# Self-attention in strips: where the reciprocals of the row sums are made and spread, and how many buffers hold them

## The chip, the cores and the metric

The kernel runs on one core of a Trainium2 chip. The metric is device time in microseconds, the median of several runs. TensorE is called PE, VectorE DVE, ScalarE ACT, GpSimd POOL, and SP is the engine that issues most DMAs. Times inside the kernel are from one profiled execution, counted from the start of its span.

## What is computed

A decoder layer on x of shape (8, 256, 512): self-attention, cross-attention and a mixture of experts, each behind a layer norm and added to x. The change touches the self-attention alone. Cut to that part:

```python
x = x + _L0_attn_ref(_layernorm(x), w_qkv, w_out)      # 16 heads of 32
    q, k, v = (qkv[:, :, 0], qkv[:, :, 1], qkv[:, :, 2])
    scores = jnp.einsum('bqhd,bkhd->bhqk', q / scale, k)
    scores = jnp.where(causal_mask[None, None], scores, NEG)
    attn = jax.nn.softmax(scores, axis=-1)
    out = jnp.einsum('bhqk,bkhd->bqhd', attn, v).reshape(b, s, HIDDEN)
    return out @ w_out
...
```

## The kernel before

The self-attention goes through the 8 batches (n) one by one, and each batch through 16 slots (h), one per head. Heads are taken in groups of four (HG). All five engines run the same list of slots, each at its own pace; what an engine does in a slot is set by lags: work with lag L that belongs to head t is done in slot t + L, and from slot 16 on in the first slots of the next batch. The order on an engine is fixed by the code; semaphores alone tie the engines together.

Per head: DVE adds the mask to the scores, negates and scales them into `prob` and takes the row maximum (L596, lag 0). POOL makes `shift` from it (L326, lag 0), ACT the exponentials and the row sums `rsum` (L397, lag 0). POOL rounds them to the upper float16 part (L333, lag 1), DVE takes the lower part (L604, lag 2), and SP issues the transposing DMA into `pt` (L255, lag 2).

Per group of four heads, on its last head's lags: PE makes all four heads' scores in the slot of the first head (L472), which waits until the maxima of the group before are read (`mx_done`), since there are only four score buffers. DVE takes the reciprocals of the row sums (`rinv`, L619, RINV_LAG), POOL spreads each over the 32 columns of its head (`rinv_wide`, L341, WIDE_LAG). PE multiplies the probabilities by v (L495, AV_LAG 7) and right behind that turns the spread reciprocals with an identity into the layout of the output (L502), for which it waits on `wide_done`. ACT copies them out of PSUM (L411), DVE multiplies the output by them (L614, lag 8), ACT rounds (L417, lag 9) and POOL takes the lower part `ot_lo` (L347, OT_LAG 9).

Between those, PE does one job in most slots: projections of q, k and v (`q`, `k`, `u`, `w`), the transposes X0 and X1 of the normalised input in slot 8, and the output products y0 and y1 in slots 10 and 11, which wait for `ot_done` of all four groups of the batch before. q0, k0, q1, k1 in slots 12 to 15 are already those of the next batch. A job's result is evacuated by ACT and, a slot later, by DVE (L575, y by L568), and three PSUM banks hold jobs, so a job waits until DVE has emptied the one three before it. POOL rounds v's lower parts two slots behind the job (L308, L310).

So PE's order in four slots is: scores, two jobs, values (L495), the turned reciprocals (L502), two jobs. Slot 10 holds the values of the batch's group 0, slot 14 those of group 1, slots 2 and 6 of the next batch those of groups 2 and 3. There is one buffer `rinv_wide`, which POOL refills after PE has read it (`r_done`).

Of the kernel before, what the change touches and what calls it, by code (L numbers as in the profile page):

```python
# [20 lines left out]
P = 128  # L21
B, S, D = 8, 256, 512
DC = D // P
TB = S // P
NT = B * TB
H, HD = 16, 32
HG = P // HD
# [8 lines left out]
def free_ap(ap, offset, dims):  # L36

    return bass.AP(tensor=ap.tensor, offset=ap.offset + offset, ap=[list(ap.ap[0])] + dims)


def wait(engine, semaphore, value):

    if not isinstance(value, int) or value > 0:
        engine.wait_ge(semaphore, value)
# [18 lines left out]
def self_attention(nc, ident, x, w_qkv, w_out, x1, xin, xr, x1_out, x1_last_out, x1_first_in,  # L63
# [9 lines left out]
    with ExitStack() as cx:  # L73
        sb = lambda n, s, d=F32: cx.enter_context(nc.sbuf_tensor(n, s, d))
# [18 lines left out]
        p_part = sb("p_part", [P, NPROB, 2, 3 * P], F16)  # L93
        pt = sb("pt", [P, NPT, 2 * 3, P], F16)
        rsum, rinv = sb("rsum", [P, G, TB, HG]), sb("rinv", [P, G, TB, HG])
        rinv_wide = sb("rinv_wide", [P, TB, HG, HD])
        o_sb = [sb(f"a_o_sb{i}", [P, S]) for i in range(2)]
        ot_hi, ot_lo = sb("ot_hi", [P, G, S], F32R), sb("ot_lo", [P, G, S], F32R)
        raw = sb("a_raw", [P, 4, DC, D])
# [16 lines left out]
        rinv_done, wide_done, av_done, r_done, rs_done = (sem(n) for n in (  # L116
            "rinv_done", "wide_done", "av_done", "r_done", "rs_done"))
# [9 lines left out]

        BANK = {j: i % 3 if i < JOBS - 1 else 1 for i, j in enumerate(ORDER)}

        HI_LAG, LO_LAG, DMA_LAG, RINV_LAG, WIDE_LAG, AV_LAG, R_LAG, ON_LAG, OT_HI_LAG, OT_LAG = 1, 2, 2, 5, 6, 7, 7, 8, 9, 9  # L130
        LO_JOB_LAG, PARTS_LAG = 1, 2

        PASSES = ((0, 0), (1, 0), (0, 1), (1, 1), (2, 0))
# [87 lines left out]
        def v_half(j):  # L221
            return slice(0, D // 2) if j[0] == "u" else slice(D // 2, D)
# [63 lines left out]
        @block.gpsimd  # L286
        def _(pool):
            nc.gpsimd.memset(expo[:], -0.5).then_inc(consts, 1)
            nc.gpsimd.memset(ident[:], 0.0).then_inc(consts, 1)
            nc.gpsimd.memset(mask[:], 0.0).then_inc(consts, 1)  # L290
            pool.wait_ge(consts, 3)
            nc.gpsimd.affine_select(out=ident[:], in_=ident[:], compare_op=ALU.not_equal, fill=1.0, base=0,
                                    pattern=[[-1, P]], channel_multiplier=1).then_inc(consts, 1)

            nc.gpsimd.affine_select(out=mask[:, P:], in_=mask[:, P:], compare_op=ALU.is_ge, fill=NEG, base=0,
                                    pattern=[[-1, P]], channel_multiplier=1).then_inc(consts, 1)

            def next_rstd(k):

                pool.wait_ge(ln_dve, k * 5 + 5)  # L300
                nc.gpsimd.tensor_tensor(rstd[:], veps[:], expo[:], ALU.pow).then_inc(ln_rstd, 1)

            def v_lower_parts(j, n):

                i, half, before = int(j[1]), v_half(j), v_at(j, n)
                pool.wait_ge(job_ev, job_at(j, n) + 1)
                pool.sem_inc(tick_pool, 1)
                nc.gpsimd.tensor_copy(v_part[1][:, i, half], v_rest[:, i, :]).then_inc(v_mid_done, 1)  # L308
                pool.wait_ge(v_mid_done, before + 1)
                nc.gpsimd.tensor_tensor(v_part[2][:, i, half], v_rest[:, i, :], v_part[1][:, i, half],  # L310
                                        ALU.subtract).then_inc(v_done, 1)

            def out_weights(c):
                if c == 0:
                    pool.wait_ge(w_in[3], 16)
                nc.gpsimd.tensor_copy(wo_hi[:, c, :], raw[:, 3, c, :]).then_inc(wo_hi_done, 1)
                pool.wait_ge(wo_hi_done, c + 1)
                nc.gpsimd.tensor_tensor(wo_lo[:, c, :], raw[:, 3, c, :], wo_hi[:, c, :].bitcast(F32),
                                        ALU.subtract).then_inc(wo_split, 1)

            def slot(n, h):
                e = head_at(h, 0, n)
                if e is not None:
                    pool.wait_ge(mx_done, n * H + h + 1)
                    pool.sem_inc(tick_pool, 1)
                    nc.gpsimd.tensor_scalar(shift[:, e, :], nmax[:, e, :], LN_UNIT, None, ALU.add).then_inc(shift_done, 1)  # L326
                t = head_at(h, HI_LAG, n)
                if t is not None:
                    pool.wait_ge(ex_done, n * H + h - HI_LAG + 1)
                    pool.sem_inc(tick_pool, 1)  # L330
                    wait(pool, pt_in[t % HG], groups_before(h, HI_LAG, n) * 16)
                    pool.sem_inc(tick_pool, 1)
                    nc.gpsimd.tensor_copy(p_part[:, t % NPROB, 0, :], prob[:, t % NPROB, :]).then_inc(p_hi_done, 1)  # L333
                g = group_at(h, WIDE_LAG, n)
                if g is not None:
                    before = groups_before(h, WIDE_LAG, n)
                    wait(pool, r_done, before)
                    pool.sem_inc(tick_pool, 1)
                    pool.wait_ge(rinv_done, before + 1)
                    pool.sem_inc(tick_pool, 1)  # L340
                    nc.gpsimd.tensor_copy(rinv_wide[:], free_ap(rinv[:, g, :, :], 0, [[HG, TB], [1, HG], [0, HD]]))\  # L341
                        .then_inc(wide_done, 1)
                g = group_at(h, OT_LAG, n)
                if g is not None:
                    pool.wait_ge(ot_hi_done, groups_before(h, OT_LAG, n) + 1)
                    pool.sem_inc(tick_pool, 1)
                    nc.gpsimd.tensor_tensor(ot_lo[:, g, :], o_sb[g % 2][:], ot_hi[:, g, :].bitcast(F32),  # L347
                                            ALU.subtract).then_inc(ot_done, 1)
                for j, of in jobs_before(h, PARTS_LAG, n):
                    if j[0] in "uw":  # L350
                        v_lower_parts(j, of)
                if h == 3 and head_at(h, 0, n) is not None and (not isinstance(n, int) or n < B - 1):
                    next_rstd(n + 1)
                if isinstance(n, int) and n == 0 and h in WO_LATER:
                    out_weights(WO_LATER[h])

            next_rstd(0)
            for h in range(H):
                slot(0, h)
            with pool.Fori(1, B - 1) as n:  # L360
                for h in range(H):
                    slot(n, h)
            for n in (B - 1, B):
                for h in range(H):
                    slot(n, h)
# [63 lines left out]
        def _(pe):  # L429
# [48 lines left out]
            def values(g, h, n):  # L478

                before, of = groups_before(h, AV_LAG, n), n if h >= AV_LAG else n - 1  # L480
# [19 lines left out]
                pe.wait_ge(wide_done, before + 1)  # L500
                for q in range(TB):
                    m = nc.tensor.matmul(o_ps[:, 1, q * P:(q + 1) * P],  # L502
                                         rinv_wide[:, q, :, :].rearrange("p j d -> p (j d)"), ident[:],
                                         start=True, stop=True)
                m.then_inc(r_done, 1)

# [1121 lines left out]
```

## Time and profile before

| | us |
|---|---|
| median of 3 runs | 865.14 |
| lowest, highest | 862.89, 865.21 |
| the profiled execution | 865.61 |
| its span, first to last instruction | 863.9 |

Busy in the span: PE 700.5 us (81%), PE weight loads 620.7, DVE 507.3 (59%), ACT 311.4, POOL 311.7 (36% each). The self-attention takes about the first 405 us, the cross-attention and the experts the rest. The second batch's first scores start at 67 us, and from there to the last batch each takes 45 us.

How to read it: a line of a timeline gives the start, the time from the first start to the last end of equal neighbours (x4 means four instructions), the engine, the line, what is written from what, and in brackets how long the engine sat idle before it and which instruction ended that. A matmul helper records its work under L58, so tiles tell one product from another. [...] A matmul's record reaches past the start of the next one, so the difference of two starts, not the length, is what one takes in a row of equal ones.

### The profile page before, as it was taken

Reading aid. Unit: us, or ns where it says so; the run is one execution under the profiler, and the core shown is the slowest. Engines: PE = TensorE matmul, PEld = TensorE weight load, DVE = VectorE, ACT = ScalarE, POOL = GpSimd, SP = SyncE. Lnnn points to the kernel's source line nnn. Section 1 sums busy time; section 2 is a strip of 40 time slices with the busy share of each in tenths; the row PEclk is TensorE's granted clock in tenths of the full one; section 3 lists DMA queues with packets and bytes.
Section 4 is the critical chain, followed back from the end, with each engine's and each line's share of the span. In section 5 each row is a group of like instructions: output and inputs, shape, how many; then the busy total and the mean of one; then the engine's idle time right before and its main releaser. Section 6 shows DMA issues by size and latency. Waiting matters only on the chain. (4 is left out here: it accounts for less than half of the span.)

```text
span 863.9 us, 19090 instructions
## 1 busy us (share of the span) xinstructions
PE 700.5 (81%) x6040; PEld 620.7 (72%) x6041; DVE 507.3 (59%) x1456; ACT 311.4 (36%) x984; POOL 311.7 (36%) x534
## 2 busy tenths in 40 slices
PE   5578787868686869665989999999999998509995
PEld 5468676858576767544878889888898997407884
DVE  4587574757666575542856465554646555554664
ACT  3455363545545454531432323131322324312221
POOL 0565454454646363641610010101010114545662
PEclk9789998989998999976799999999999999758999
DMA  9166463545454444741942131212223124516630
GB/s 345 48 109 84 86 126 79 130 89 121 97 112 97 105 80 88 133 107 51 353 180 98 50 98 49 97 51 94 73 73 98 48 73 141 152 43 203 198 120 24
DMA packets 142885, 95.07 MB, mean 110 GB/s; under 512 B 110846, under 2 KB 115070, under 8 KB 142720
## 3 DMA queue, kind: packets, MB, share of 16 engines
q1 hardware_dynamic: 137184, 82.00, 36.6%
q0 software_dynamic: 5664, 12.61, 4.7%
q8 instruction: 19, 0.31, 0.2%
q14 instruction: 18, 0.15, 0.1%
HBM read 56.14 MB, written 18.77 MB: 87 GB/s over the span
## 5 line engine op out<-in xcount | busy, mean ns | idle before, releaser
L397 ACT ACTIVATE prob<-prob,shift 128x128 f32<-128x128 f32 (+1 forms) x256 | 114.5, 449 | 170.4 <-POOL shift L326 170.4
L58 PE MATMUL b_bank<-w_hi 128*128 128x256 f32 (+1 forms) x576 | 119.9, 331 | 7.2 <-DVE w_lo L1187 7.2
L999 ACT CAST w_hi<-b_bank 128x256 fp32r<-128x256 f32 (+1 forms) x144 | 60.2, 445 | 161.0 <-PE b_bank L58 143.2
L58 PE MATMUL b_bank<-w_lo,w_hi 128*128 128x256 f32 (+1 forms) x576 | 114.8, 322 | 0.0
L58 PE MATMUL b_bank<-w_hi,w_lo 128*128 128x256 f32 (+1 forms) x576 | 114.7, 322 | 0.0
L596 DVE CUSTOM_DVE_ANT_0 prob<-a_s,mask 128x128 f32<-128x128 f32 (+1 forms) x256 | 79.2, 347 | 49.2 <-PE a_s L472 48.9
L604 DVE TENSOR_TENSOR p_part<-prob,p_part 128x384 f16<-128x384 f32 x128 | 79.7, 622 | 42.9 <-POOL p_part L333 42.7
L58 PEld LDWEIGHTS b_bank<-w_hi 128*128 128x128 f32 x576 | 90.1, 196 | 15.7 <-DVE w_lo L1187 7.8
L58 PEld LDWEIGHTS b_bank<-w_lo,w_hi 128*128 128x128 f32 x576 | 90.8, 194 | 8.0
L1187 DVE TENSOR_TENSOR w_lo<-b_bank,w_hi 128x256 fp32r<-128x256 f32 (+1 forms) x144 | 68.4, 508 | 47.4 <-ACT w_hi L999 47.3
L58 PEld LDWEIGHTS b_bank<-w_hi,w_lo 128*128 128x128 f32 x576 | 90.7, 194 | 7.6
L326 POOL TENSOR_SCALAR shift<-nmax 128x2 f32<-128x2 f32 x128 | 42.4, 332 | 137.5 <-DVE nmax L596 126.7
L502 PE MATMUL a_o<-ident,rinv_wide 128*128 128x128 f32 x128 | 27.9, 351 | 68.3 <-POOL rinv_wide L341 68.3
L502 PEld LDWEIGHTS a_o<-ident,rinv_wide 128*128 128x128 f32 x128 | 20.7, 230 | 75.8 <-POOL rinv_wide L341 75.5
L333 POOL CAST p_part<-prob 128x384 f16<-128x384 f32 x128 | 64.3, 503 | 8.7 <-ACT prob L397 0.7
L58 PE MATMUL a_job<-a_xt_hi,wqkv_hi 128*128 128x256 f32 x256 | 45.4, 301 | 7.9 <-DVE q_part L575 2.8
L397 ACT ACTIVATION_READ_ACCUMULATOR prob<-prob,shift 128x1 f32 x256 | 48.1, 188 | 0.0
L955 POOL TENSOR_TENSOR b_rstd<-b_veps,b_expo 128x2 f32<-128x2 f32 x8 | 6.1, 757 | 112.9 <-DVE b_veps L1165 112.9
L58 PEld LDWEIGHTS a_job<-a_xt_hi,wqkv_hi 128*128 128x128 f32 x256 | 35.6, 196 | 12.1 <-DVE wqkv_lo L560 4.2
L347 POOL TENSOR_TENSOR ot_lo<-a_o_sb,ot_hi 128x256 fp32r<-128x256 f32 x32 | 25.0, 781 | 47.3 <-ACT ot_hi L417 47.3
L58 PE MATMUL a_job<-a_xt_lo,wqkv_hi 128*128 128x256 f32 x256 | 41.0, 284 | 0.0
L58 PE MATMUL a_job<-a_xt_hi,wqkv_lo 128*128 128x256 f32 x256 | 40.9, 283 | 0.0
(169 smaller groups left out, 1360.0 us busy)
## 6 DMA issues: line engine op xcount, KB each, us to landing
stage<-in_w SPq DMA_DIRECT2D x8, 1024.0 KB, 5.5
xin<-in_x SPq DMA_DIRECT2D x8, 512.0 KB, 4.1
xr<-in_x SPq DMA_DIRECT2D x8, 512.0 KB, 4.2
x<-xr SPq DMA_DIRECT2D x8, 512.0 KB, 3.2
xin<-x SPq DMA_DIRECT2D x8, 512.0 KB, 4.6
b_cin_t<-in_ctx_t SPq DMA_DIRECT2D x8, 512.0 KB, 3.6
b_cin<-in_ctx SPq DMA_DIRECT2D x8, 512.0 KB, 3.5
xr<-x SPq DMA_DIRECT2D x8, 512.0 KB
```

The source lines that it names most:

```text
L58: ins = pe_matmul(out, a, b, start=first and i == 0, stop=last and i == len(steps) - 1)
L326: nc.gpsimd.tensor_scalar(shift[:, e, :], nmax[:, e, :], LN_UNIT, None, ALU.add).then_inc(shift_done, 1)
L333: nc.gpsimd.tensor_copy(p_part[:, t % NPROB, 0, :], prob[:, t % NPROB, :]).then_inc(p_hi_done, 1)
L347: nc.gpsimd.tensor_tensor(ot_lo[:, g, :], o_sb[g % 2][:], ot_hi[:, g, :].bitcast(F32), ALU.subtract).then_inc(ot_done, 1)
L397: a = nc.scalar.activation(prob[:, e % NPROB, cols], prob[:, e % NPROB, cols], ACT.Exp, scale=-1.0, bias=shift[:, e, q:q + 1], accum_out=r ...
L502: m = nc.tensor.matmul(o_ps[:, 1, q * P:(q + 1) * P], rinv_wide[:, q, :, :].rearrange("p j d -> p (j d)"), ident[:], start=True, stop=True)
L596: m = nc.vector.tensor_tensor_reduce(out=prob[:, s % NPROB, cols], in0=s_ps[s % HG][:, q, 0:P * (q + 1)], in1=mask[:, P * (1 - q):], scale ...
L604: nc.vector.tensor_tensor(p_part[:, t % NPROB, 1, :], prob[:, t % NPROB, :], p_part[:, t % NPROB, 0, :], ALU.subtract).then_inc(p_done, 1)
L955: nc.gpsimd.tensor_tensor(rstd[:, 0, :], veps[:, 0, :], expo[:], ALU.pow).then_inc(ln_rstd, 1)
L999: nc.scalar.copy(hi, src).then_inc(job_hi, 1)
L1187: nc.vector.tensor_tensor(lo, src, hi.bitcast(F32), ALU.subtract).then_inc(job_ev, 1)
```

## The change

Three things, all in `self_attention`.

1. RINV_LAG goes from 5 to 2 and WIDE_LAG from 6 to 3. The last head of a group has number 3, 7, 11 or 15, so DVE takes the reciprocals in slots 1, 5, 9, 13 and not in 0, 4, 8, 12 of the group after, and POOL spreads them in slots 2, 6, 10, 14 that follow the group at once, where it had done so in slots 1, 5, 9, 13 one group later.
2. `rinv_wide` becomes two buffers, taken in turn by the group's number.
3. POOL's copy waits for `r_done` of one group fewer, since the buffer it fills was read two groups ago.

AV_LAG stays 7: PE reads the spread values where it did.

```diff
-        rinv_wide = sb("rinv_wide", [P, TB, HG, HD])
+        rinv_wide = [sb(f"rinv_wide{i}", [P, TB, HG, HD]) for i in range(2)]
...
-        HI_LAG, LO_LAG, DMA_LAG, RINV_LAG, WIDE_LAG, AV_LAG, R_LAG, ON_LAG, OT_HI_LAG, OT_LAG = 1, 2, 2, 5, 6, 7, 7, 8, 9, 9
+        HI_LAG, LO_LAG, DMA_LAG, RINV_LAG, WIDE_LAG, AV_LAG, R_LAG, ON_LAG, OT_HI_LAG, OT_LAG = 1, 2, 2, 2, 3, 7, 7, 8, 9, 9
...
-                    wait(pool, r_done, before)
+                    wait(pool, r_done, before - 1)
                     pool.sem_inc(tick_pool, 1)
                     pool.wait_ge(rinv_done, before + 1)
                     pool.sem_inc(tick_pool, 1)
-                    nc.gpsimd.tensor_copy(rinv_wide[:], free_ap(rinv[:, g, :, :], 0, [[HG, TB], [1, HG], [0, HD]]))\
+                    nc.gpsimd.tensor_copy(rinv_wide[g % 2][:], free_ap(rinv[:, g, :, :], 0, [[HG, TB], [1, HG], [0, HD]]))\
                         .then_inc(wide_done, 1)
...
-                                         rinv_wide[:, q, :, :].rearrange("p j d -> p (j d)"), ident[:],
+                                         rinv_wide[g % 2][:, q, :, :].rearrange("p j d -> p (j d)"), ident[:],
```

On POOL, in the loop's slots 5 and 6, the old place of the copy and the new one. Each pair of L326 and L333 is one head: shift of this slot, upper part of the head before. L308 and L310 are v's lower parts.

```order
@@ -91,8 +92,8 @@
 L44 ISA
 L333 CAST p_part<-prob 128x384
-L341 COPY rinv_wide<-rinv 128x256
-L324 REGISTER_ALU
-L326 TENSOR_SCALAR shift<-nmax 128x2
-L333 CAST p_part<-prob 128x384
+L324 REGISTER_ALU
+L326 TENSOR_SCALAR shift<-nmax 128x2
+L333 CAST p_part<-prob 128x384
+L341 COPY rinv_wide<-rinv 128x256
 L306 REGISTER_ALU
 L308 CAST v_part<-v_rest 128x256
```

The copy moved from behind slot 5's upper part to behind slot 6's, so it now stands right ahead of v's lower parts. It belongs to another group too: in slot 6 it is that of heads 0 to 3, in slot 5 it had been that of the batch before's heads 12 to 15.

On DVE, in the loop's slots 4 and 5; L596 and its reads are a head's maximum, L604 the lower part, L575 an evacuation.

```order
@@ -178,13 +178,13 @@
 L570 REGISTER_ALU
 L575 TENSOR_TENSOR k_part<-a_job,k_part 128x256
+L596 ISA prob,nmax<-a_s,mask 128x128
+L596 ISA nmax 128x1
+L596 ISA prob,nmax<-a_s,mask 128x256
+L596 ISA nmax 128x1
+L604 TENSOR_TENSOR p_part<-prob,p_part 128x384
+L570 REGISTER_ALU
+L575 TENSOR_TENSOR v_rest<-a_job,v_part 128x256
 L618 ISA
 L619 RECIPROCAL rinv<-rsum 128x8
```

The reciprocals moved one head back within the four slots, from ahead of the second head's maximum to ahead of the third's.

## Rows read from the trace of the kernel before

**Rows 1.** The list of waits, 0 to 450 us: us in total, times, longest us

```profile
PE a_o L502 <- POOL rinv_wide L341: 68.3, 31, 5.2
```

**Rows 2.** Busy time by stretch: PE, PEld, DVE, ACT, POOL, then granted clock, DMA

```profile
195.00:240.00 45.00, 35.80 (x456) 31.60 (x456) 29.56 (x111) 22.37 (x86) 23.24 (x49) 0.96 0.48 105
```

**Rows 3.** Timeline of PE, one batch: start us, length us, line, work, [idle before]

```profile
203.99 0.96 PE L472 MATMUL a_s<-k_part,q_part 32*128 32x128 f32 x24
...
210.28 0.71 PE L502 MATMUL a_o<-ident,rinv_wide 128*128 128x128 f32 x4 [0.83 <-POOL rinv_wide L341]
...
213.75 0.96 PE L472 MATMUL a_s<-k_part,q_part 32*128 32x128 f32 x24
...
220.25 0.71 PE L502 MATMUL a_o<-ident,rinv_wide 128*128 128x128 f32 x4 [1.59 <-POOL rinv_wide L341]
...
223.72 0.96 PE L472 MATMUL a_s<-k_part,q_part 32*128 32x128 f32 x24
...
225.63 1.01 PE L495 MATMUL a_o<-pt,v_part 128*32 128x256 f16 x40
231.72 1.22 PE L502 MATMUL a_o<-ident,rinv_wide 128*128 128x128 f32 x4 [5.08 <-POOL rinv_wide L341]
232.60 2.05 PE L58 MATMUL a_job<-wout_hi,ot_hi 128*128 128x512 f32 x4
...
235.59 1.08 PE L58 MATMUL a_job<-wout_hi,ot_lo 128*128 128x512 f32 x4
...
239.35 0.96 PE L472 MATMUL a_s<-k_part,q_part 32*128 32x128 f32 x24
...
245.59 0.71 PE L502 MATMUL a_o<-ident,rinv_wide 128*128 128x128 f32 x4 [1.41 <-POOL rinv_wide L341]
...
248.97 0.96 PE L472 MATMUL a_s<-k_part,q_part 32*128 32x128 f32 x24
```

**Rows 4.** Timeline of DVE, the same batch

```profile
219.88 0.72 DVE L604 TENSOR_TENSOR p_part<-prob,p_part 128x384 f16<-128x384 f32 x1 [0.93 <-POOL p_part L333]
...
222.00 0.08 DVE L596 DVE_READ_ACCUMULATOR2_ANT nmax<- 128x1 f32 x1
...
246.81 0.08 DVE L596 DVE_READ_ACCUMULATOR2_ANT nmax<- 128x1 f32 x1
...
257.73 0.08 DVE L596 DVE_READ_ACCUMULATOR2_ANT nmax<- 128x1 f32 x1
```

**Rows 5.** Timeline of POOL, the same batch

```profile
219.80 0.40 POOL L341 COPY rinv_wide<-rinv 128x256 f32<-128x256 f32 x1
...
224.03 0.68 POOL L310 TENSOR_TENSOR v_part<-v_rest,v_part 128x256 bf16<-128x256 f32 x1
225.84 0.35 POOL L326 TENSOR_SCALAR shift<-nmax 128x2 f32<-128x2 f32 x1 [1.13 <-DVE nmax L596]
...
228.65 0.73 POOL L347 TENSOR_TENSOR ot_lo<-a_o_sb,ot_hi 128x256 fp32r<-128x256 f32 x1 [1.90 <-ACT ot_hi L417]
```

**Rows 6.** The same, one microsecond of the first batch

```profile
54.00:55.00 1.00, 0.03 (x1) 0.03 (x1) 1.00 (x5) 0.96 (x4) 0.94 (x4) 0.50 1.11 82
```

**Rows 7.** Timeline of PE, first batch

```profile
54.97 1.22 PE L502 MATMUL a_o<-ident,rinv_wide 128*128 128x128 f32 x4 [2.27 <-POOL rinv_wide L341]
56.34 1.66 PE L472 MATMUL a_s<-k_part,q_part 32*128 32x128 f32 x24
...
63.80 0.71 PE L502 MATMUL a_o<-ident,rinv_wide 128*128 128x128 f32 x4 [0.60 <-POOL rinv_wide L341]
```

**Rows 8.** Timeline of PE, last batch

```profile
359.89 0.96 PE L472 MATMUL a_s<-k_part,q_part 32*128 32x128 f32 x24
...
367.09 1.22 PE L502 MATMUL a_o<-ident,rinv_wide 128*128 128x128 f32 x4 [5.22 <-POOL rinv_wide L341]
...
375.26 0.96 PE L472 MATMUL a_s<-k_part,q_part 32*128 32x128 f32 x24
...
383.76 1.79 PE L495 MATMUL a_o<-pt,v_part 128*32 128x256 f16 x40 [1.73 <-DMA pt<-p_part]
```
## The prediction

> **Names.** A batch of the self-attention has 16 slots, one per head. Slots 0 to 3 are strip A, 4 to 7 strip B, 8 to 11 strip C, 12 to 15 strip D. Each strip opens on PE with the scores of its four heads (L472). "S" is the start of those scores; a strip's length runs from its S to the next one.
>
> **What bounds the kernel now.** I read the list of waits of the first 450 us first. PE stood for 68.3 us in 31 waits before the matmuls of L502, the ones that turn the spread reciprocals, and POOL's copy of L341 ended all of them [rows 1]. The busy times by stretch say whether that engine matters there: in a stretch of 45 us, which is one batch, PE is busy 35.80 us, DVE 29.56, POOL 23.24, ACT 22.37 [rows 2]. PE idles 9.2 us of a batch, so a wait of PE is time as long as nothing else is nearly as full. Then the timeline of PE, strip by strip [rows 3]: before L502 it waits 0.83 us in strip A, 1.59 in B, 5.08 in C and 1.41 in D, 8.9 us together, which is all of its idle time but 0.3. Strip lengths are A 9.76 us (203.99 to 213.75), B 9.97 (to 223.72), C 15.63 (to 239.35), D 9.62 (to 248.97), 44.98 together. The work queued behind the waiting matmuls, two projections or the two output products and then the next scores, is what starts late, and with the scores DVE's next four heads.
>
> **What the change removes.** The copy for a group now stands four slots and more before PE asks for it: POOL makes it in slot 2 of the strip before, PE reads it in slot 2 of the next. POOL can't be that far behind, since PE's next scores themselves wait for the last head's maxima of the strip before. So the wait at L502 goes in every strip, and the question is what is late next. Two things are, and I work both out for each strip: PE's own work (length less the wait), and DVE's last maximum of the strip, for which the next scores wait, plus about 0.15 us until they start (in the first batch the maximum was the later one, and the scores began at 56.34 [rows 7]).
>
> Strip A: PE 9.76 - 0.83 = 8.93. DVE: the last maximum is read at 257.73 + 0.08, that is S + 8.84 for S = 248.97 [rows 3, 4], so 9.0. I take 8.95: **0.8 us less**.
>
> Strip B: PE 9.97 - 1.59 = 8.38; DVE 222.00 + 0.08 - 213.75 = 8.33, with the hand-over 8.5 [rows 3, 4]. **1.5 less**. Both limits are within 0.15 us of each other: from here on more speed on PE alone would bring nothing.
>
> Strip D: PE 9.62 - 1.41 = 8.21; DVE 246.81 + 0.08 - 239.35 = 7.54. PE's last projection needs a bank that DVE empties one head earlier than the last; that comes some 0.2 us too late for the shorter strip, an estimate from the same timeline. I take 8.4: **1.2 less**.
>
> Strip C is where most lies, and where not all of it can be had. Without the wait PE does the copy's matmuls right behind the values, and then the output product of L454 waits for the lower part of the attention's output, L347 on POOL, which ended at 228.65 + 0.73 = 229.38, S + 5.66 [rows 3, 5]. Before, that was hidden behind the later wait. It also comes a little later against S: POOL's head shift at 225.84 had waited 1.13 us for DVE; it now comes 1.45 us earlier (strip B's gain), while POOL is held until 224.71 by the lower parts of v (224.03 + 0.68), and by 0.25 us more, because the moved copy of 0.40 us stands ahead of them and only some 0.15 us of it falls into time in which POOL waited for the exponential [rows 5]. So shift starts 0.6 us later after S, and the product at S + 5.66 + 0.6 + 0.1 = 6.35. The two products took 6.75 us (232.60 to 239.35) at a clock that had fallen in the wait of 5.08 us; at the full clock four matmuls take 0.94 us (235.59 to 239.35 are four such rows), six rows 5.64 [rows 3]. So strip C is 12.0 us long with the full clock (3.6 less) and 13.1 with the low one (2.5 less). PE would stand some 2.2 us before the product. [...] I take the middle, **3.0 less**.
>
> **The sum.** A batch is 0.8 + 1.5 + 3.0 + 1.2 = 6.5 us shorter, and there are six whole ones (slot 0 of the second to slot 0 of the eighth): 39 us. In the eighth, A and B give 2.3, and of C's wait of 5.22 us [rows 8] about 1.1 stays before the product, since it needs L347 all the same: 4.1. Its strip D gives nothing: from S = 375.26 the chain goes through the last heads and their transposing DMAs, and PE waits for pt at 383.76 [rows 8]. The first batch gives 0.6 of strip D [rows 7] and nothing of C, whose scores began at 56.34 although the wait had ended 1.4 us earlier: they waited for the maximum. 39 + 2.3 + 4.1 + 0.6 = **46 us**. What comes behind the self-attention starts from its end and is the same. The profiled execution took 865.61 us (span 863.9), so 819.6; the median of the three runs is 0.5 lower, 819.1. I say 819.
>
> **Costs beside it.** The reciprocal (a slot later in its strip, 0.19 us) stays ahead of the same last maximum, and its input is long there: zero, at most 0.1 us a strip. The copy's new wait (r_done of the group before last) is met a whole strip before. The copy no longer stands ahead of POOL's shift of slot 2, and stands ahead of the one of slot 3: from -0.4 to +0.4 us on one head's chain, 31 times, -12 to +12 us, if that chain were the only limit. I take zero, since in A and B the heads of slot 2 and 3 are followed by DVE's own work until the maximum, and in C and D PE is the limit. The transposing DMAs move with the heads. Of v's lower parts the first values of a batch need the second one; it comes at S + 2.7 in strip C, 0.6 us after PE could use it, before the longer wait for L347, so it costs nothing.
>
> One row bears on that bound. DVE's lower part of slot 2 took 0.72 us at 219.88 and had started beside the copy of 219.80 [rows 4, 5]. [...]
>
> **Rivals.** *B: the heads' chain takes the wait over.* DVE's idle time at the start of a strip now lets it finish the strip before. Shorter strips could push that work (lower part, an evacuation, the product with the reciprocals) past the end of the scores, and POOL with it. For it: the two limits of A and B are nearly equal already, and DVE waited 0.93 us for POOL inside strip B [rows 4]. Against it: DVE is busy 29.56 of 45 us [rows 2]. If A, B and D lose another 1.0 us each, seven batches give 21 us back: 840. *C: no change.* The label names the last of several things, and the transposed probabilities or v come at the same time: 865. Against it: behind the values nothing but the copy is left for L502, and values ran 5 us ahead in strip C [rows 3]. *D: slower.* The copy stands ahead of slot 3's shift and of v's lower parts on POOL. If the PE wait is only moved to the next scores, as in the first batch's strip C [rows 7], each strip pays the copy: 32 x 0.40 = 12.8 us, 878. It decides as soon as the last maximum, not PE, ends every strip and POOL's copy lies on its path. *E: more.* Full clock in every strip C and no loss anywhere: 7.1 x 6 + 7.5 = 50, and 3 us from shorter stretches of low clock behind it: 812.
>
> **How the numbers follow.** Forecast 0.66 (813 to 827), B 0.18, E 0.07, C 0.05, D 0.04. The range leaves out C, D and the slower part of B: 808 to 838, where 838 is B with nine tenths of its price. A measurement here tells 0.3%, 2.6 us, from no change. Faster: 0.66 + 0.18 + 0.07 = 0.91 and nothing of C; same 0.05; slower 0.04.
>
> **What would show it.** PE's waits for rinv_wide gone from the list of waits, in the list in their place: PE for ot_lo, about 2.2 us in each strip C, and scores that wait for the last maximum in A and B. Lengths of A 8.95, B 8.5, C 12.0 to 13.1, D 8.4, a batch 38 to 39 us. The granted clock in strip C says which of the two lengths holds. POOL's L308 behind L341 in slot 2 of strip B. The forecast is wrong if batches stay above 41 us; then the row before the scores names what took over.

## The result, and the profile after

| | us | of before |
|---|---|---|
| before, median of 4 | 864.85 (862.89 to 865.21) | |
| changed, median of 4 | 822.42 (819.07 to 825.95) | 0.9514, 95% interval 0.9469 to 0.9559 |
| changed, the profiled execution | 825.95, span 824.2 | |

The kernel became 42 us faster. The profiled execution is the slowest of its four, which turns out to matter below.

In the list of PE's groups over the first 410 us, the matmuls of L502 have lost their whole idle time (0.0 us behind the bar, where [rows 1] had 68.3), and are shorter (311 ns each, where it had been 351). Of their 32 groups of four, ten took 1.14 to 1.22 us before, two take 1.22 now, and nearly all others take 0.71. The one of [rows 3] with 1.22 us, at 231.72, ran at a granted clock of 0.50, counted as a share of full speed:

```profile
L502 PE MATMUL a_o<-ident,rinv_wide 128*128 128x128 f32 x128 | 23.8, 311 | 0.0
```

What PE waits for in their place, in the list of waits of the first 410 us (total, times, longest):

```profile
PE a_job L58 <- POOL ot_lo L347: 14.1, 8, 2.3
...
PE a_o L495 <- DMA pt<-p_part: 10.3, 2, 6.0
...
PE a_o L495 <- POOL v_part L310: 7.9, 8, 1.5
```

PE's values (L495) wait for the DMAs twice, at the end of the last batch. The page's table of costly groups has one more wait that matters here: DVE waits 32.2 us for POOL's upper part, where it had waited 42.7:

```profile
L604 DVE TENSOR_TENSOR p_part<-prob,p_part 128x384 f16<-128x384 f32 x128 | 80.8, 631 | 33.2 <-POOL p_part L333 32.2
```

One batch by its own stretch, from the scores of slot 0 to the next ones. PE is busy as long as before [rows 2], in 39.31 us, not 45, that is 91% of it (this is the shortest of the six batches):

```profile
189.11:228.42 39.31, 35.89 (x449) 31.45 (x448) 30.18 (x112) 22.14 (x87) 23.26 (x50) 0.96 0.54 120
```

PE's timeline of that batch, for [rows 3]. Strips begin at 189.11, 198.10, 206.46, 219.79 and 228.42:

```profile
189.11 0.96 PE L472 MATMUL a_s<-k_part,q_part 32*128 32x128 f32 x24
...
198.10 0.96 PE L472 MATMUL a_s<-k_part,q_part 32*128 32x128 f32 x24
...
206.46 0.96 PE L472 MATMUL a_s<-k_part,q_part 32*128 32x128 f32 x24 [0.17 <-issue]
...
209.33 1.01 PE L495 MATMUL a_o<-pt,v_part 128*32 128x256 f16 x40 [0.89 <-POOL v_part L310]
210.27 0.71 PE L502 MATMUL a_o<-ident,rinv_wide 128*128 128x128 f32 x4
212.78 2.07 PE L58 MATMUL a_job<-wout_hi,ot_hi 128*128 128x512 f32 x4 [1.80 <-POOL ot_lo L347]
214.65 1.55 PE L58 MATMUL a_job<-wout_lo,ot_hi 128*128 128x512 f32 x4
...
219.79 0.96 PE L472 MATMUL a_s<-k_part,q_part 32*128 32x128 f32 x24
...
226.85 0.74 PE L58 MATMUL a_job<-a_xt_hi,wqkv_hi 128*128 128x256 f32 x4 [0.16 <-DVE k_part L575]
...
228.42 0.96 PE L472 MATMUL a_s<-k_part,q_part 32*128 32x128 f32 x24
```

The reader is to see three things. L502 stands right behind the values now (210.27, and in the other strips without a wait). The output product waits for ot_lo until 212.78, 6.32 us after the scores at 206.46. And its first rows are long: 2.07 and 1.55 us for four matmuls that take 0.92 from start to start from 216.03 on.

All strips of the two profiled executions, worked out from the starts of L472 in such timelines; strip C is split at the start of the output products:

```
us            A (0-3)  B (4-7)   C until products + products      D (12-15)
before        9.6-9.8  9.9-10.0  8.8-8.9 + 6.8 to 8.2 (mean 7.4)   9.6
changed       9.0      8.35      6.3     + 7.0 to 8.6 (mean 7.9)   8.6
changed, eighth batch
              8.8      8.3       5.1     + 5.7
```

### The profile page after: what moved, and what is told of

Read it like the earlier page. It is cut to its first block and busy times, and to the rows that moved or that the text cites. A ratio compares the mean times of both kernels' runs of the same rounds, so it can differ in the third digit from the quotient of the medians.

```text
span 824.2 us, 19084 instructions
## 1 busy us (share of the span) xinstructions
PE 701.5 (85%) x6040; PEld 621.1 (75%) x6041; DVE 512.8 (62%) x1456; ACT 310.1 (38%) x984; POOL 311.8 (38%) x534
## 5 line engine op out<-in xcount | busy, mean ns | idle before, releaser
L604 DVE TENSOR_TENSOR p_part<-prob,p_part 128x384 f16<-128x384 f32 x128 | 80.8, 631 | 33.2 <-POOL p_part L333 32.2
L596 DVE CUSTOM_DVE_ANT_0 prob<-a_s,mask 128x128 f32<-128x128 f32 (+1 forms) x256 | 79.4, 347 | 34.2 <-PE a_s L472 34.1
L1187 DVE TENSOR_TENSOR w_lo<-b_bank,w_hi 128x256 fp32r<-128x256 f32 (+1 forms) x144 | 68.3, 507 | 46.1 <-ACT w_hi L999 46.0
L326 POOL TENSOR_SCALAR shift<-nmax 128x2 f32<-128x2 f32 x128 | 45.6, 356 | 98.2 <-DVE nmax L596 90.9
L333 POOL CAST p_part<-prob 128x384 f16<-128x384 f32 x128 | 64.3, 503 | 8.7 <-ACT prob L397 0.7
L495 PE MATMUL a_o<-pt,v_part 128*32 128x128 f16 (+1 forms) x1280 | 33.8, 254 | 18.2 <-DMA pt<-p_part 10.3
L955 POOL TENSOR_TENSOR b_rstd<-b_veps,b_expo 128x2 f32<-128x2 f32 x8 | 6.1, 756 | 111.2 <-DVE b_veps L1165 111.2
L495 PEld LDWEIGHTS a_o<-pt,v_part 128*32 128x32 bf16 x1280 | 26.0, 99 | 23.6 <-issue 20.3
L959 POOL TENSOR_TENSOR b_rstd<-b_veps,b_expo 128x2 f32<-128x2 f32 x8 | 5.6, 697 | 96.4 <-DVE b_veps L1165 96.3
L1468 ACT CAST c_xt_hi<-c_bank 128x512 fp32r<-128x512 f32 x23 | 13.5, 587 | 74.3 <-PE c_bank L1488 74.3
L347 POOL TENSOR_TENSOR ot_lo<-a_o_sb,ot_hi 128x256 fp32r<-128x256 f32 x32 | 23.4, 730 | 47.5 <-ACT ot_hi L417 47.5
```

Source lines behind the costliest of these rows:

```text
L495: m = nc.tensor.matmul(o_ps[j * HD:(j + 1) * HD, 0, seen], v_part[a][:, k, at:at + HD], pt[:, (g * HG + j) % NPT, 3 * z + blocks.start:3 * ...
L596: m = nc.vector.tensor_tensor_reduce(out=prob[:, s % NPROB, cols], in0=s_ps[s % HG][:, q, 0:P * (q + 1)], in1=mask[:, P * (1 - q):], scale ...
L604: nc.vector.tensor_tensor(p_part[:, t % NPROB, 1, :], prob[:, t % NPROB, :], p_part[:, t % NPROB, 0, :], ALU.subtract).then_inc(p_done, 1)
L1187: nc.vector.tensor_tensor(lo, src, hi.bitcast(F32), ALU.subtract).then_inc(job_ev, 1)
L1468: nc.scalar.copy(xt_hi[:, k % 2, :], t_ps[k % 2][:, :]).then_inc(xt_hi_done, 1)
```

## The experiments

All took the same inputs; unless a text says otherwise they compute the whole layer. Strips were read from each run's trace in the way of the table above.

### Which part of the change brings it

Both halves alone. First the new lags with one buffer:

```diff
-        HI_LAG, LO_LAG, DMA_LAG, RINV_LAG, WIDE_LAG, AV_LAG, R_LAG, ON_LAG, OT_HI_LAG, OT_LAG = 1, 2, 2, 5, 6, 7, 7, 8, 9, 9
+        HI_LAG, LO_LAG, DMA_LAG, RINV_LAG, WIDE_LAG, AV_LAG, R_LAG, ON_LAG, OT_HI_LAG, OT_LAG = 1, 2, 2, 2, 3, 7, 7, 8, 9, 9
```

> The new lags (2 and 3) with the one rinv_wide buffer of before, so POOL's copy waits until PE has read the copy of the group before. Theory 1 (the place of the copy is all that matters): PE reads at about 4.8 us after a strip's first scores and POOL reaches the copy at about 6.7 us in strip B, so the wait costs nothing and the time is that of the changed kernel, 822 us, within 2 us. Theory 2 (the second buffer is needed, since the copy now stands in the same slot as PE's read): PE and POOL wait for each other, the heads behind the copy come 0.5 us or more later in each of 31 groups, 838 us or more.

Measured: 823.16 us median (815.26 to 827.7), ratio 0.9542 (0.9495 to 0.9588). A 9.0, B 8.36, the products at 6.33, D 8.64, all as in the changed kernel. Theory 1 holds: the place of the copy is all, and the second buffer brings nothing that these runs can tell. POOL waited for PE to free the one buffer once, for 1.6 us, in the last batch.

Then two buffers with the lags of before:

> The lags of before (5 and 6) with two buffers in turn. Theory 1: nothing moves, PE's waits for rinv_wide stay at 68 us in 31 waits, and the time is that of before, 865 us, within 3. If the one buffer had held POOL back, these waits and the time would fall; the gain of two buffers alone would then be a part of the 42 us.

Measured: 864.47 us (one run) beside 864.51 of before, strips A 9.7, B 9.9, C 15.6 to 17.0, D 9.7, and 68.5 us in 31 waits of PE for rinv_wide. The buffer alone does nothing.

The run with one buffer also shows what its own median hides. Its products took 5.7 us in four of the six whole batches of the profiled execution (815.26 us) and 7.3 in the others, where the changed kernel's took 7.0 to 8.6 in all six (825.95 us). Everything else in the whole batches is the same to 0.05 us.

### What makes the output products of strip C long

Busy time by microsecond of the changed kernel's strip C; the granted clock is the figure behind POOL's count:

```profile
211.00:212.00 1.00, 0.00 (x0) 0.00 (x0) 1.00 (x2) 0.74 (x2) 0.07 (x1) 1.00 0.70 134
212.00:213.00 1.00, 0.22 (x1) 0.23 (x2) 0.89 (x6) 0.00 (x0) 0.99 (x2) 0.61 0.95 190
213.00:214.00 1.00, 1.00 (x3) 0.81 (x4) 0.00 (x0) 0.00 (x0) 0.85 (x2) 0.50 0.04 7
...
216.00:217.00 1.00, 1.00 (x6) 0.80 (x5) 0.20 (x1) 0.77 (x3) 0.94 (x3) 1.00 0.33 68
```

PE had ended L502 by 211.0 and stood until 212.78. The granted clock was 1.00 until 212.2, while PE stood, 0.50 from 212.3 on, 0.48 us before the products began, and 1.00 again at 216. So that PE has no such gap, the turning matmuls of group 0 are done five times over:

```diff
-                for q in range(TB):
+                for q in [0, 1] * (5 if g == 0 else 1):
                     m = nc.tensor.matmul(o_ps[:, 1, q * P:(q + 1) * P],
```

> The changed kernel, with the two turning matmuls of group 0 done five times over (same result), so that PE works through the 1.8 us in which it waits for ot_lo ahead of the output products of strip C. If the low granted clock there is what makes the two products take 7.0 to 8.6 us instead of 5.6, and it falls because of PE's idle time, strip C goes from 13.3 to 14.9 us down to 12 to 12.6 and the time to 808 to 814 us. If the clock falls all the same, the time stays at 822 to 824. If the products are long for another reason, such as waits for their operands, the records keep their length at granted clock 1.00.

Measured: 809.26 us (807.41 to 811.1), ratio 0.9361 (0.932 to 0.9401), 13 us under the changed kernel. PE's timeline of one strip C:

```profile
198.65 0.96 PE L472 MATMUL a_s<-k_part,q_part 32*128 32x128 f32 x24
...
202.46 2.50 PE L502 MATMUL a_o<-ident,rinv_wide 128*128 128x128 f32 x20
204.99 1.19 PE L58 MATMUL a_job<-wout_hi,ot_hi 128*128 128x512 f32 x4
206.01 1.08 PE L58 MATMUL a_job<-wout_lo,ot_hi 128*128 128x512 f32 x4
...
210.69 0.96 PE L472 MATMUL a_s<-k_part,q_part 32*128 32x128 f32 x24
```

The products start 6.34 us after the scores, as in the changed kernel, and take 5.7 us in all seven batches, at a granted clock of 1.00: 1.02 us from the first row's start to the second's, about 0.92 for the others. Strip C is 12.04 us in all six whole batches. The time that work without a result fills is not lost, since PE would have stood.

The same in the kernel before, with 20 products of the output weights into the bank that y0 overwrites, behind the values of group 0:

```diff
                 m.then_inc(av_done, 1)
+                if g == 0 and has("y0", n):
+                    pe.wait_ge(job_ev, job_at(*last_in_bank("y0", n)) + 1)
+                    for i in range(20):
+                        nc.tensor.matmul(bank("y0")[:, :], wo_hi[:, i % DC, 0:P], wo_hi[:, i % DC, :], start=True, stop=True)
                 pe.wait_ge(wide_done, before + 1)
```

> The kernel before, with 20 idle products of the output weights behind the values of group 0, into the bank that the output product overwrites, so that PE works through 4.5 of the 5.1 us in which it waits for rinv_wide in strip C. It splits the gain. If the low clock behind that wait costs what the spread of strip C says (15.6 to 17.0 us, of which 8.9 until the product starts, so 6.7 to 8.1 where full clock needs 5.6), strip C becomes 14.5 and the time 850 to 856 us: then 10 to 14 us of the distance between the kernel before and the one with the fed clock, 864.5 to 809.3, is clock and the rest waiting. If the filling work is too long or the bank comes late, strip C starts its product later than 8.9 us after its scores and the gain is smaller.

Measured: 847.69 us (845.89 to 850.12), ratio 0.9826 (0.9791 to 0.9861). Less than 2%, but clear of the seven runs of before beside it (860.88 to 866.7).

```profile
217.32 0.96 PE L472 MATMUL a_s<-k_part,q_part 32*128 32x128 f32 x24
...
220.17 4.83 PE L503 MATMUL a_job<-wout_hi 128*128 128x512 f32 x20
225.36 0.71 PE L506 MATMUL a_o<-ident,rinv_wide 128*128 128x128 f32 x4 [0.36 <-POOL rinv_wide L341]
225.83 1.17 PE L58 MATMUL a_job<-wout_hi,ot_hi 128*128 128x512 f32 x4
...
231.51 0.96 PE L472 MATMUL a_s<-k_part,q_part 32*128 32x128 f32 x24
```

Products of 5.69 us in all seven batches, at a granted clock of 1.00, against a mean of 7.4: 7 x 1.7 = 12 us. They start 0.37 us earlier, 2.6 us more: L502 takes 0.71 us at 225.36, at a granted clock of 1.00, where [rows 3] had 1.22. The whole was 16.3 us (864.0 to 847.7), a little more than I expected. The distance between the two kernels with PE fed is 847.7 - 809.3 = 38.4 us. That is what the change brings with the clock of strip C taken out of both, so it is waiting. Left to itself the change brings 42 us, since the kernel before loses 16.3 us to that clock and the changed one 13.2 (822.4 to 809.3).

### What ends strips A and B

```diff
                     dve.wait_ge(ex_done, before * HG + HG)
+                    nc.vector.reciprocal(rinv_again[:], rsum[:, g, :, :])
                     nc.vector.reciprocal(rinv[:, g, :, :], rsum[:, g, :, :]).then_inc(rinv_done, 1)
```

> The changed kernel, with each reciprocal on DVE done twice (the first into a spare tile). Theory: strips A and B now end with DVE's last maximum, C and D with PE. Then A grows from 9.00 and B from 8.36 by one reciprocal, 0.11 to 0.19 us, and C's start of the output product and D's 8.63 stay. Rival: PE's own work ends A and B too (its sum was 8.93 and 8.38); then A and B stay within 0.03 us.

Measured: 821.98 us (one run). A 9.00 and B 8.36 in every whole batch, products at 6.33, D 8.63. My expectation failed: one more reciprocal on DVE ahead of the last maximum moved nothing. That left PE, or a chain that DVE itself waits on. So PE was made lighter; this kernel leaves out one of the three passes of the projections:

```diff
-                                   ([w_hi[:, c, cols] for c in chunks], [w_lo[:, c, cols] for c in chunks]))
+                                   ([w_hi[:, c, cols] for c in chunks], [w_lo[:, c, cols] for c in chunks]), passes=2)
...
-                                   ([xt_hi[:, c, :] for c in chunks], [xt_lo[:, c, :] for c in chunks]))
+                                   ([xt_hi[:, c, :] for c in chunks], [xt_lo[:, c, :] for c in chunks]), passes=2)
```

> The changed kernel, with one of the three passes (lower part of the left operand times upper part of the right) left out of the projections of q, k and v, so those are less exact. Each is 0.45 us shorter, which takes 1.8 us of PE's work from strips A, B and D. Doubling the reciprocals on DVE had not moved A and B, so either PE ends them after all (then they fall to about 7.2 and 6.6 us and the time by over 20 us), or the heads' chain over POOL and ACT does, which had room for a second reciprocal while DVE waited for POOL (then A stays at 9.00 and B at 8.36 within 0.1, strip C's product still starts at 6.3, and D falls until its last maximum ends it, from 8.63 to about 7.7). By the second the time falls by 7 to 8 us at the same draws of the clock, and the granted clock may fall more often, since PE idles more.

Measured: 810.69 us (one run). A 8.99 and B 8.36 stay although PE has 1.8 us less to do in each, so PE does not end them. D fell to 8.17 only, since its last projection waits for the bank that DVE empties (k_part in the list below; 1.5 us in strip D). PE's starts of scores, and the waits of 60 to 300 us:

```profile
183.78 0.96 PE L473 MATMUL a_s<-k_part,q_part 32*128 32x128 f32 x24
...
192.77 0.96 PE L473 MATMUL a_s<-k_part,q_part 32*128 32x128 f32 x24 [1.50 <-DVE nmax L597]
...
201.14 0.96 PE L473 MATMUL a_s<-k_part,q_part 32*128 32x128 f32 x24 [2.00 <-issue]
```

```profile
PE a_s L473 <- DVE nmax L597: 9.0, 6, 1.5
...
PE a_job L59 <- DVE k_part L576: 14.5, 13, 1.6
```

The row at 201.14 names no releaser, but the last maximum's read ended 0.10 us ahead of it. So the heads' chain ends A and B. DVE's timeline of the changed kernel, whose scores start at 189.11 (A), 198.10 (B) and 206.46 (C), shows how it runs:

```profile
195.03 0.56 DVE L604 TENSOR_TENSOR p_part<-prob,p_part 128x384 f16<-128x384 f32 x1 [0.45 <-POOL p_part L333]
...
196.07 0.68 DVE L541 BATCH_NORM_STATS2 a_stats<-xin 128x6 f32<-128x512 f32 x1
196.67 0.41 DVE L548 BATCH_NORM_AGGREGATE a_mv<-a_stats 128x2 f32<-128x6 f32 x2
197.12 0.17 DVE L550 TENSOR_SCALAR a_veps<-a_mv 128x2 f32<-128x2 f32 x1
...
197.87 0.08 DVE L596 DVE_READ_ACCUMULATOR2_ANT nmax<- 128x1 f32 x1
...
203.99 0.56 DVE L604 TENSOR_TENSOR p_part<-prob,p_part 128x384 f16<-128x384 f32 x1
...
206.28 0.08 DVE L596 DVE_READ_ACCUMULATOR2_ANT nmax<- 128x1 f32 x1
```

The first row is slot 2 of strip A, with the wait for POOL (0.45 us) into which a second reciprocal disappears: in that run the wait is 0.39 and the row starts 5.92 us after the scores, as here. Behind it DVE works without a pause of more than 0.14 us until the last maximum, read 8.84 us after the scores; in strip B it is 8.26 us. The next scores start 0.15 and 0.10 us after the ends of these reads. So strip A ends by POOL until slot 2 and by DVE's own work behind it, and part of that work is the next batch's layer norm (L541 to L550, 1.24 us from 196.07 to 197.31, where the last maximum begins). The eighth batch tells this: it has no such rows, and with the lighter PE its A and B are 7.65 and 7.62 us. DVE in its strip A, whose scores start at 296.43:

```profile
302.30 0.56 DVE L605 TENSOR_TENSOR p_part<-prob,p_part 128x384 f16<-128x384 f32 x1 [1.05 <-POOL p_part L334]
...
303.90 0.08 DVE L597 DVE_READ_ACCUMULATOR2_ANT nmax<- 128x1 f32 x1
```

The lower part starts 5.87 us after the scores, as ever, but the last maximum's read ends 1.68 us behind it and not 2.92. So a reciprocal on DVE ahead of the wait for POOL costs nothing, and the layer norm behind it is what the strip's length holds.

### Where the copy is best placed

Twice the copy, the first into a spare tile, in slot 2:

> The changed kernel, with POOL's copy made twice (the first into a spare tile), 0.35 to 0.4 us more in slot 2 of each strip. If my account of its place holds, A, B and D stay (the copy lies behind the upper part for which DVE waits), the first batch's third strip, which ends with its last maximum, grows by 0.4, and in strip C the output product starts 0.35 to 0.4 later than 6.3 us after the scores, 7 times: 2.5 to 3 us in all. If the copy stood on the chain of all strips, the time grows by 31 x 0.4 = 12 us.

Measured: 818.3 us, one run, with products of 5.7 us, at a granted clock of 1.00, in four of seven batches; that clock is why the time lies under the changed kernel's, and the strips are what to compare. A 9.00, B 8.36 and D 8.63 stay; the products start at 6.85, not 6.33, and the first batch's third strip, which ends with its last maximum, is 8.72 us, not 8.11 to 8.26 as in the runs with one copy in slot 2. One more copy costs strip C 0.5 us, a little more than I expected, and the other strips of a whole batch nothing. POOL's timeline of the changed kernel, for [rows 5]:

```profile
205.13 0.40 POOL L341 COPY rinv_wide<-rinv 128x256 f32<-128x256 f32 x1
...
208.31 0.67 POOL L310 TENSOR_TENSOR v_part<-v_rest,v_part 128x256 bf16<-128x256 f32 x1
209.06 0.40 POOL L326 TENSOR_SCALAR shift<-nmax 128x2 f32<-128x2 f32 x1
...
211.93 0.72 POOL L347 TENSOR_TENSOR ot_lo<-a_o_sb,ot_hi 128x256 fp32r<-128x256 f32 x1 [1.90 <-ACT ot_hi L417]
```

The copy of slot 6 is at 205.13, v's lower part ends at 208.98, and shift of slot 8 starts 0.08 later: POOL is late for strip C, and L347 with it.

So the copy goes where POOL waits anyway, ahead of L347 in slot 0 of the next strip (lag 5), one buffer, and the reciprocal into slot 3 (lag 4):

```diff
-        HI_LAG, LO_LAG, DMA_LAG, RINV_LAG, WIDE_LAG, AV_LAG, R_LAG, ON_LAG, OT_HI_LAG, OT_LAG = 1, 2, 2, 5, 6, 7, 7, 8, 9, 9
+        HI_LAG, LO_LAG, DMA_LAG, RINV_LAG, WIDE_LAG, AV_LAG, R_LAG, ON_LAG, OT_HI_LAG, OT_LAG = 1, 2, 2, 4, 5, 7, 7, 8, 9, 9
```

> One buffer, reciprocals in slot 3 behind the last maximum (lag 4), copy in slot 0 of the next strip (lag 5), where POOL waits about 1.2 us for ot_hi. PE reads it in slot 2. If POOL's place of the copy matters as I argued (it delays v's lower parts and the shift of strip C), strip C becomes 0.3 us shorter than in the changed kernel and strips A and B 0.1 us, since the reciprocals leave the path to the maximum: 819 to 821 us. If lead is what counts, the copy comes at 3.5 us after the strip's start and PE asks at 3.8 to 4.8, so PE waits again in strip C, and the time is 823 or more.

Measured: 813.28 us (811.24 to 814.05), ratio 0.9405 (0.9366 to 0.9444), better than expected. The products start at 5.93, not 6.33, and kept the full clock in five of the six whole batches (5.7 us at a granted clock of 1.00, against 7.28 us at a mean of 0.77 in the sixth). A is 9.0. B is longer, 8.59, so the places of copy and reciprocal alone give some 0.2 us a batch (0.4 less in C, 0.2 more in B); most of the 9 us is the clock. PE's gap ahead of the products is 1.64 us here and not 1.80; that this is why the clock held more often is not shown. In B, L347 and DVE's L554 ran into each other; POOL first, DVE below:

```profile
192.99 0.40 POOL L341 COPY rinv_wide<-rinv 128x256 f32<-128x256 f32 x1
194.24 1.01 POOL L347 TENSOR_TENSOR ot_lo<-a_o_sb,ot_hi 128x256 fp32r<-128x256 f32 x1 [0.85 <-ACT ot_hi L417]
```

```profile
194.12 0.54 DVE L554 TENSOR_SCALAR a_xn<-xin,a_mv,a_rstd 128x512 f32<-128x512 f32 x1
```

L347 took 1.01 us, not 0.72, with L554 just started. In the kernel before it had been so too (the last section has the row). With the reciprocal back in slot 1, ahead of L554, and PE fed as above:

> One buffer, copy in slot 0 of the next strip (lag 5) as in the run with lags 4 and 5, reciprocals in slot 1 as in the changed kernel (lag 2), and PE kept busy before the output products by the repeated turning matmuls of group 0. With lags 4 and 5 strip C took 11.63 where the clock held and strip B 8.59, since POOL's L347 ran into DVE's L554 (1.01 us instead of 0.72). If it is the reciprocal ahead of L554 that lets L347 start first, strip B comes back to 8.36 and a batch takes 9.0 + 8.36 + 11.63 + 8.64 = 37.6: 805 to 807 us. If B stays at 8.6, 808.

Measured: 807.38 us (806.07 to 807.81), ratio 0.9347 (0.9315 to 0.9379). B is 8.36 again, C 11.63, the batch 37.64 us: 0.4 us less than the 38.04 of the fed kernel with the copy in slot 2, and 1.9 us less in all.

### What the output product waits for

L347 waits for ACT's rounding (L417), which stood behind the job's evacuation. Here it goes ahead of it, in all strips; else the changed kernel:

```diff
+                g = group_at(h, OT_HI_LAG, n)
+                if g is not None:
...
+                    nc.scalar.copy(ot_hi[:, g, :], o_sb[g % 2][:]).then_inc(ot_hi_done, 1)
                 for j in jobs_of(h, n):
                     if j not in LATE:
                         evac(j, n)
...
-                g = group_at(h, OT_HI_LAG, n)
-                if g is not None:
...
-                    nc.scalar.copy(ot_hi[:, g, :], o_sb[g % 2][:]).then_inc(ot_hi_done, 1)
```

> The changed kernel, with ACT rounding the attention's output (L417) ahead of the job's evacuation in the same slot. In strip C it stood behind the two transposed inputs (1.05 us). If L347 on POOL is what the output product of strip C waits for, the product starts at 5.3 to 5.5 us after the scores and not at 6.3, and PE's idle time there shrinks from 1.8 to about 0.8, so that the clock may stay up as well: 810 to 817 us. A and B: L347 also stands ahead of the upper part for which DVE waits 0.2 to 0.9 us, so they may gain 0.1. Rival: the transposed input's evacuation is needed first and C does not move; 820 or more.

Measured: 803.94 us (802.95 to 806.0), ratio 0.9314 (0.928 to 0.9349). PE's timeline of one strip C, whose scores start at 194.47:

```profile
197.20 1.01 PE L495 MATMUL a_o<-pt,v_part 128*32 128x256 f16 x40 [0.75 <-POOL v_part L310]
...
199.69 1.19 PE L58 MATMUL a_job<-wout_hi,ot_hi 128*128 128x512 f32 x4 [0.84 <-POOL ot_lo L347]
...
205.40 0.96 PE L472 MATMUL a_s<-k_part,q_part 32*128 32x128 f32 x24
```

The products start at 5.23, PE's gap ahead of them is 0.84 us and not 1.80, and they took 5.7 us in all seven batches, at a granted clock of 1.00, without any filling work. A became 8.84, B 8.32 and D 8.4: L347 stands on the chain ahead of slot 2's upper part. The time is below the 810 to 817 that I expected, which had only strip C move by 1 us and left the clock open. Both edits together:

> One buffer, reciprocals in slot 1 (lag 2), copy in slot 0 of the next strip (lag 5), and ACT's rounding of the output ahead of the evacuation. If the 0.4 us that the copy's place cost strip C is still there once the rounding is early, C goes from 10.93 to 10.5 us and the time from 804 to 801. If POOL then waits in slot 0 for nothing, so that the copy stands on the way to L347, C keeps 10.9 and A and B grow: 804 to 806.

Measured: 800.58 us (799.97 to 801.58), ratio 0.9269 (0.9234 to 0.9304). Products at 4.82, C 10.5, a batch 36.05 us. This is the best version run, 22 us under the changed kernel, with the one buffer of before.

## Why the prediction was right

The prediction was 819 us in a range of 808 to 838, and 822.4 was measured. Its forecast, not a rival, is what happened: the wait at L502 went, strips A, B, D and the start of the products came within 0.25 us of what was worked out for them, and PE waited for ot_lo in strip C. How near the time came is in part luck. The two profiled executions differ by 39.7 us, the medians by 42.4, and 46 was forecast; and two executions with the same strips but for the clock of strip C took 815.3 and 825.95 us. Point by point:

- **What bounds the kernel, and that the wait goes.** Right. 68.3 us of waits at L502 became 0.0, and 38.4 us of the gain is there with the low clock of strip C taken out of both kernels.
- **Strip A, 8.95.** 9.00 measured, by the last maximum, as the sum had it. The chain to it is POOL's until slot 2 and DVE's own work behind that, as the costs said; the reciprocal stands ahead of the wait for POOL, so that its cost is zero, as forecast, though not only because "its input is long there".
- **Strip B, 8.5.** 8.35. The last maximum was read at 8.26 us and not 8.33, and its hand-over took 0.10 us and not 0.15.
- **Strip C until the product, 6.35.** 6.32. The parts hold too: the values waited 0.89 us for v's lower parts, the product 1.80 us for L347, where the text has "some 2.2".
- **Strip C, the products.** Here a term was mis-sized. The low clock was priced from one batch at 6.75 us, and the seven batches of before spread from 6.75 to 8.16 (mean 7.39), at mean granted clocks of 0.83 to 0.67; that one was the cheapest. For the same reason the whole batches took 44.98 to 46.38 us and not 45 each. I took the middle between 5.64 and 6.75, 6.2, and no run shows it: behind a gap of 1.8 us the products took 5.7 to 5.8 us at a granted clock of 1.00 (four of the six whole batches with one buffer) or 7.0 us and more at a mean of 0.80 and less (all six of the changed kernel). The changed kernel's profiled run had 7.0 to 8.6, mean 7.9, in the whole batches, so strip C gave 2.1 us (16.3 to 14.2), not 3.0. In whole batches that is 5.4 us where 6.5 was forecast (273.4 us from slot 0 of the second to slot 0 of the eighth batch before, 241.0 after: 32.4 us and not 39). Another execution of nearly the same instructions (one buffer) had four of six batches at the full clock, so that a median nearer to the forecast than the profiled time is no merit of the sum.
- **Strip D, 8.4.** 8.63. The bank wait was there, at 226.85: this row starts 0.80 us after the one before it, where the same rows elsewhere take 0.47. The cost was 0.4 in all (8.63 against PE's 8.21) and not 0.2; 0.1 of it is not traced.
- **The first batch, 0.6 less.** Wrong: from its first scores to the second batch's it took 47.43 us before and 47.45 after. Strip D gave its 0.6 (10.85 to 10.29), but B took 0.1 more, and the third strip, which ends with its last maximum, 0.4 more (7.7 to 8.1), since the copy now stands on that chain. This is rival D's mechanism, in the one strip of 31 where it holds, and doubling the copy made it 8.7.
- **The eighth batch, 6.4 less.** 6.8 (34.7 to 27.9). Strip D gave nothing, as said: the first values come 8.5 us after its scores before and 8.6 after, and PE waits longer for pt.

```profile
336.65 0.96 PE L472 MATMUL a_s<-k_part,q_part 32*128 32x128 f32 x24
...
345.22 1.79 PE L495 MATMUL a_o<-pt,v_part 128*32 128x256 f16 x40 [6.03 <-DMA pt<-p_part]
...
352.44 1.79 PE L495 MATMUL a_o<-pt,v_part 128*32 128x256 f16 x40 [4.28 <-DMA pt<-p_part]
```

- **What comes behind, the same.** Only to some us: from the scores of the eighth batch's strip D to the end it took 488.6 us before, 487.6 after, and 483.0 to 490.7 in all thirteen profiled executions.
- **The copy's new place, zero.** Right for A, B and D. In C 0.25 us were counted for it; one more copy there costs 0.5, and taking it out of slot 2 gave 0.4.
- **DVE's row beside the copy.** It took 0.72 us [rows 4], and takes 0.56 at 195.03 and 203.99, where the copy has gone. The next DVE instruction still starts 0.70 us after it, in strip B by a wait for ACT's evacuation, so no strip gained from it. Beside the copy's new place L554 took 0.77 us at 205.04, where it had taken 0.59 at 220.93, but 0.77 too in the run that has the copy in slot 0.
- **Rival B** did not come: DVE finished the strip before while the scores ran, and idled 1.28 us ahead of strip A's first maximum. **Rival E** wanted the full clock in every strip C; that is the run with PE fed, 809.

What stays open is why the clock holds in one batch and falls in the next with the same 1.80 us gap. In the whole batches it always held where the gap ahead of the products was 0.84 us or less, or filled. That is no safe length. In the eighth batches, where the values wait longer for v_part (1.4 to 1.5 us, not 0.9), a gap of 0.97 us was followed by products of 5.7 us (changed kernel), 7.1 (one buffer) and 8.6 (reciprocals twice), and with lags 4 and 5 waits of 1.39, 0.30 and 0.43 us by products of 6.9 us; PE's row there, and its busy time by microsecond with the granted clock at 0.50:

```profile
316.69 2.07 PE L58 MATMUL a_job<-wout_hi,ot_hi 128*128 128x512 f32 x4 [0.43 <-POOL ot_lo L347]
```

```profile
317.00:318.00 1.00, 1.00 (x3) 0.81 (x3) 0.00 (x0) 0.00 (x0) 0.86 (x2) 0.50 1.16 235
```

## What to carry to other kernels

When a wait of the bounding engine is removed, work out for each stretch what that engine waits for next, and give the stretch that length; the order of the late things here (ot_lo, last maximum, PE itself) was readable from rows of before, to 0.05 us for strip A and the start of the products, to 0.15 for B and 0.23 for D. A step ahead of the last wait of an engine can be made longer for nothing (a second reciprocal of 0.19 us left A at 9.00 and B at 8.36 us), one behind it can't be told by that test (the layer norm, 1.24 us). Look at the clock of the matmuls behind each remaining gap, over all repeats of the stretch and not one, for here it was worth as much as the gap: 13.2 us in the changed kernel, where the gaps of strip C were 6 x 1.80 + 0.97 = 11.8 us. And before adding a buffer, ask whether an earlier place alone does it: a copy belongs in a slot where its engine waits anyway (0.4 us of each strip C here), and a short rounding (0.41 us) ahead of a long evacuation (1.05 us) when another engine's next step hangs on it (the products start at 5.23 us and not 6.33).

## What was not expected of the hardware

The granted clock in strip C differed with equal instructions and an equal gap of 1.8 us: the two products took 5.7 to 5.8, 7.0 to 7.3, or 8.4 to 8.6 us, at mean granted clocks of 1.00, 0.77 to 0.80, and 0.64 to 0.65, which makes one execution differ from the next (815.26 and 825.95 us for the profiled ones of the kernel with one buffer and of the changed one). It does not look like plain chance. The kernel before and the one with two buffers and the old lags have the same strip lengths within 0.1 us, and their products took 6.96, 8.16, 7.29, 6.75, 8.06, 7.21, 7.29 us and 6.88, 8.12, 7.22, 6.73, 8.08, 7.22, 7.31, batch by batch. What sets this course no run shows. With the gap filled, or ACT's rounding early (a gap of 0.84 or 0.67 us in the whole batches), they took 5.7 us at a granted clock of 1.00 in all batches seen, and those kernels' runs lie within 1.6 to 4.2 us.

POOL's L347 took 1.01 us where DVE's L554 had started 0.12 us ahead of it, in the run with lags 4 and 5 and in the kernel before:

```profile
217.98 1.01 POOL L347 TENSOR_TENSOR ot_lo<-a_o_sb,ot_hi 128x256 fp32r<-128x256 f32 x1 [1.20 <-ACT ot_hi L417]
```

In both L554 took 0.54. In the changed kernel, with the reciprocal ahead of L554, the two start together and it is the other way round: L347 takes 0.72 and L554 1.01 (0.73 and 0.95 in the run with the reciprocals twice, where L347 starts 0.06 us ahead). So it goes in strip B of all whole batches of the thirteen profiled executions: with L554 0.11 to 0.12 us ahead, L347 took 1.00 to 1.01 us and L554 0.54; with L554 between 0.02 us ahead and 0.06 behind, 0.72 to 0.74 and 0.95 to 1.03; with it 0.56 to 0.57 behind, in the two runs with ACT's rounding early, 0.73 to 0.74 and 0.49 to 0.50. Between the runs with lags 4 and 5 and with lags 2 and 5, moving a reciprocal of 0.19 us by two slots turned it round, at 0.23 us in each strip B; the change moves the reciprocal too, which the prediction had counted as zero.
